# A graph network on one core: the loaded rows of a dense pair added by VectorE in PSUM instead of by a matmul, the output constant added in VectorE's copy

## What is computed

```python
h = jnp.maximum(_layernorm(x, axis=-1), 0.0)
x = x + _L0_gnn_ref(h, ...)      # three graph convolutions and a product
h = jnp.maximum(_layernorm(x, axis=-1), 0.0)
x = x + _L1_gnn_ref(h, ...)      # mean of edges, two products with batch norms
h = jnp.maximum(_layernorm(x, axis=-1), 0.0)
x = x + _L2_gnn_ref(h, ...)      # six steps x += relu(mean of neighbours @ W.T + b)
h = jnp.maximum(_layernorm(x, axis=-1), 0.0)
x = x + _L3_gnn_ref(h, ...)      # tanh(graph convolution) @ W2 + b2
```

## Time and profile before

| | us |
|---|---|
| median of three runs | 3292.27 |
| lowest and highest | 3290.51, 3295.48 |
| the profiled execution | 3287.36 |
| its span | 3285.6 |

### The profile page before, as it was taken

The page is one execution under the profiler, slowest core; times in us unless marked ns, Lnnn a source line. Parts: engine busy times, 40 slices in busy tenths (PEclk is TensorE's granted clock), DMA queues, the critical chain, the costliest instruction groups (busy, mean ns, idle before and its releaser), DMA issues. The chain is left out here.

```text
span 3285.6 us, 46019 instructions
## 1 busy us (share of the span) xinstructions
PE 2527.2 (77%) x11251; PEld 1564.2 (48%) x11251; DVE 2032.4 (62%) x7784; ACT 1972.3 (60%) x4381; POOL 1442.2 (44%) x1507
## 2 busy tenths in 40 slices
PE   5767755558777678899999945799999999876840
PEld 2444434435555456445455422365655656543520
DVE  6544555558889766233333356687887878776630
ACT  1666755557777766455555558877777776764400
POOL 5555454545645264000000000176766767554576
PEclk8888877789888898899999966899999999987875
DMA  4655533445566565333333458866656656433311
GB/s 94 173 158 154 170 109 111 121 119 163 165 179 195 173 193 168 108 137 134 137 134 134 137 183 268 282 186 185 192 177 189 186 175 191 146 116 112 96 57 41
DMA packets 528965, 504.91 MB, mean 154 GB/s; under 512 B 58706, under 2 KB 389955, under 8 KB 528616
## 3 DMA queue, kind: packets, MB, share of 16 engines
q1 hardware_dynamic: 477388, 415.73, 39.2%
q0 software_dynamic: 47184, 85.73, 10.5%
q10 hardware_dynamic: 4172, 0.99, 0.2%
HBM read 246.45 MB, written 260.27 MB: 154 GB/s over the span
## 5 line engine op out<-in xcount | busy, mean ns | idle before, releaser
L1854 POOL DMA_INDIRECT h_G<-step_tab,row_i x294 | 287.1, 977 | 350.1 <-DMA step_tab<-l_NR 192.9
L1854 POOL DMA_INDIRECT h_M<-step_tab,row_i x294 | 284.3, 967 | 119.3 <-issue 86.3
L1567 DVE TENSOR_SCALAR b_Y<-b_BP,col 128x512 f32<-128x512 f32 x148 | 109.9, 742 | 354.5 <-PE b_BP L1521 354.5
L804 PE MATMUL a_PA<-a_H,w 128*128 128x512 f32 x504 | 263.2, 650 | 70.2 <-ACT a_H L968 63.4
L1549 ACT ACTIVATE b_Z<-b_BQ,bn 128x512 f32<-128x512 f32 x148 | 115.0, 777 | 256.7 <-PE b_BQ L1513 256.4
L1521 PE MATMUL b_BP<-b_Z,w 128*128 128x512 f32 x592 | 266.3, 592 | 0.0
L1609 POOL TENSOR_TENSOR b_d<-b_d,neghalf 128x1 f32<-128x1 f32 x1 | 0.6, 565 | 592.4 <-DVE b_d L1600 592.4
L2221 DVE TENSOR_TENSOR_SCAN h_T<-keep,h_T,h_P 128x512 f32<-128x512 bf16 x196 | 222.9, 1137 | 11.3 <-PE h_P L1972 2.1
L270 POOL DMA_INDIRECT h_G<-msg_tab,row_i x147 | 143.8, 978 | 195.5 <-issue 132.1
L239 ACT ACTIVATE a_NR<-a_XR,a_ln_nm,a_ln_rs 128x128 f32<-128x128 f32 x392 | 155.9, 485 | 106.3 <-DVE a_ln_nm L222 106.3
L239 ACT ACTIVATE a_HI<-a_X,a_ln_nm,a_ln_rs 128x128 f32<-128x128 f32 x490 | 201.0, 484 | 23.2 <-DVE a_ln_nm L222 23.2
(11 more groups left out here) (385 smaller groups left out, 6503.9 us busy)
## 6 DMA issues: line engine op xcount, KB each, us to landing
b_HI<-hin_tab SPq DMA_DIRECT2D x148, 256.0 KB, 2.8
y_tab<-b_Y SPq DMA_DIRECT2D x148, 256.0 KB, 2.0
l_Y<-y_tab SPq DMA_DIRECT2D x148, 256.0 KB, 4.0
l_X<-x_tab SPq DMA_DIRECT2D x148, 256.0 KB, 4.6
x_tab<-a_X SPq DMA_DIRECT2D x112, 256.0 KB, 4.3
hin_tab<-a_HI SPq DMA_DIRECT2D x112, 256.0 KB, 3.1
a_XR<-in_x SPq DMA_DIRECT2D x97, 256.0 KB, 4.5
out_rows<-l_O SPq DMA_DIRECT2D x97, 256.0 KB, 3.1
```

Of the source, the lines that this page charges most:

```text
L804: nc.tensor.matmul(PA[b][:, 0:nt * P], w[:, :], h[b][:, 0:nt, :].rearrange("p t d -> p (t d)"), start=True, stop=True).then_inc(done, 1)
L1567: nc.vector.tensor_scalar(Y[b][:, :], BP[b][:, :], col[:, C_B12:C_B12 + 1], None, ALU.add).then_inc(b_y, 1)
L1854: pool.indirect_dma_start(out=GR_[i % 2][b][:, k, :], out_offset=None, in_=table[:, :], in_offset=bass.IndirectOffsetOnAxis(ap=row_i[:, t ...
```

## The change

PE no longer adds the loaded rows and the output constant for dense pairs. `add_x1` and `rows_const` go (a matmul of 128x512 floats and a bf16 matmul for each of 98 banks). In `x2(j)` DVE now adds `X1` to the bank in place, one 128x512 `tensor_tensor` a bank that reads and writes PSUM, after `turned` and `x1_in`, and raises `x2_bank` itself; PE's later matmuls go on adding to the bank. In `rows_out` the copy becomes a `tensor_tensor` that adds a resident broadcast `rb32` of `b32`. `rb32` is loaded at the start by one more DMA in ACT's queue.

```diff
--- before.py
+++ after.py
@@ -141,6 +141,7 @@
     col = sb(top, "col", [P, 12])
     C_B01, C_B02, C_B31, C_B12, C_GA2, C_BE2, C_B11, C_GA1, C_BE1 = 0, 1, 2, 3, 4, 5, 6, 8, 10
     rbh = sb(top, "rbh", [P, D])
+    rb32 = sb(top, "rb32", [P, D])
     split_x1 = sb(top, "split_x1", [3, 512], BF16)
     split_out = sb(top, "split_out", [3, 512], BF16)
     split_r6 = sb(top, "split_r6", [3, 512], BF16)
@@ -494,7 +495,7 @@
     feat_in, feat_pad, mh_st, mh_ones = sems("feat_in", 2), sem("feat_pad"), sems("mh_st", 2), sem("mh_ones")
     FULL = NT - 1
     REST = E - FULL * P
-    N_LOADS = 29
+    N_LOADS = 30
     padded = [(t, base) for t in (hin_tab, x1_tab) for base in (E0, S0)]
     padded += [(t, base) for t in msg_tab[1:] + step_tab + [last_tab] for base in (0, RR)]
 
@@ -917,6 +918,7 @@
         def _(act):
             loads = [(w3[:, :], W03[:, :]), (wl[:, :], W0l[:, :]), (whs[:, :], Wh[:, :]), (b3col[:, :], column(b03)), (bhcol[:, :], column(bh)),
                      (rbl[:, :], b0l.partition_broadcast(P)), (rbh[:, :], bh.partition_broadcast(P)),
+                     (rb32[:, :], b32.partition_broadcast(P)),
                      (w01[:, :], W01[:, :]), (w02[:, :], W02[:, :]),
                      (w31[:, :], W31[:, :]), (w32[:, :], W32[:, :]), (w11[:, :], W11[:, :]),
                      (w12[:, :, :], W12.rearrange("(c p) n -> p c n", p=P)),
@@ -1913,12 +1915,6 @@
                             last = nc.tensor.transpose(turned_in(j, b)[:, k * P:(k + 1) * P], Y[j % 2][b][:, k, :], ident[:, :])
                     last.then_inc(turned, 1)
 
-            def add_x1(j):
-                for b in range(2):
-                    pe.wait_ge(x1_in[j % 2][b], 16 * (j // 2 + 1))
-                    nc.tensor.matmul(XB[j % 2][b][:, :], ident[:, :], X1[j % 2][b][:, :, :].rearrange("p t d -> p (t d)"), start=False,
-                                     stop=True, skip_group_check=True).then_inc(x2_bank, 1)
-
             def x3(j):
                 for b in range(2):
                     if full(j, b):
@@ -1946,17 +1942,13 @@
                     pe.wait_ge(h_set, n + 1)
                     nc.tensor.matmul(PC[b][:, :], w31[:, :], HT[b][:, :, :].rearrange("p t d -> p (t d)"), start=True, stop=True).then_inc(p1_set, 1)
 
-            def rows_const(j):
-                for b in range(2):
-                    nc.tensor.matmul(XB[j % 2][b][:, :], ones3[:, :], split_out[:, :], start=False, stop=False, skip_group_check=True)
-
             def rows(j):
                 for b in range(2):
                     n = 2 * (j - D0) + b
                     pe.wait_ge(tanh_set, n + 1)
                     pc_user[b] = (tanh_set, n + 1)
                     for k in range(4):
-                        last = nc.tensor.matmul(XB[j % 2][b][:, k * P:(k + 1) * P], HT[b][:, k, :], w32[:, :], start=False, stop=(k == 3), skip_group_check=True)
+                        last = nc.tensor.matmul(XB[j % 2][b][:, k * P:(k + 1) * P], HT[b][:, k, :], w32[:, :], start=False, stop=True, skip_group_check=True)
                     last.then_inc(p2_set, 1)
 
             def hop_turn(i):
@@ -2011,8 +2003,6 @@
                 j, its = sl.pair, sl.its
                 if j is not None:
                     turn(j)
-                    if is_d(j):
-                        add_x1(j)
                 if j is not None and MIX < j <= D0:
                     x3(j - 1)
                 for i in its[:1]:
@@ -2020,8 +2010,6 @@
                 if late is not None:
                     turn2(late)
                     prod(late)
-                if late is not None:
-                    rows_const(late)
                 for i in its[:1]:
                     if i < F0:
                         hop_blocks(i, (0,))
@@ -2153,11 +2141,13 @@
         def _(dve):
             def x2(j):
                 for b in range(2):
-                    if is_d(j):
-                        continue
                     q, r, n = 2 * j + b, j % 2, width(j, b)
                     dve.wait_ge(turned, q + 1)
                     dve.wait_ge(x1_in[r][b], 16 * (j // 2 + 1))
+                    if is_d(j):
+                        bank = XB[r][b][:, :].rearrange("p (t d) -> p t d", d=D)
+                        nc.vector.tensor_tensor(bank, X1[r][b][:, :, :], bank, ALU.add).then_inc(x2_bank, 1)
+                        continue
                     if full(j, b):
                         if j >= 2 and full(j - 2, b):
                             dve.wait_ge(x3_sum, no2(j - 2, 0) + no2(j - 2, 1) + (b + 1 if j - 2 > MIX else 1))
@@ -2191,7 +2181,8 @@
                     r = j % 2
                     dve.wait_ge(p2_set, 2 * (j - D0) + b + 1)
                     dve.wait_ge(o_st[b], o_stores(j, b))
-                    nc.vector.tensor_copy(O[b][:, :, :].rearrange("p t d -> p (t d)"), XB[r][b][:, :]).then_inc(o_set, 1)
+                    nc.vector.tensor_tensor(O[b][:, :, :], XB[r][b][:, :].rearrange("p (t d) -> p t d", d=D),
+                                            rb32[:, :].unsqueeze(1).broadcast_to([P, 4, D]), ALU.add).then_inc(o_set, 1)
 
             def rstd2(j):
                 j2 = j - MIX
```

## The result

| | us |
|---|---|
| changed kernel, median of 12 runs | 3300.26 (3290.73 to 3306.73) |
| kernel before, median of 12 runs beside it | 3290.70 (3286.74 to 3298.97) |
| ratio, 95% interval | 1.0023 (1.0013 to 1.0033) |
| span of the profiled execution | 3302.2 (before 3285.6) |

The change costs 0.23%, some 8 us; the forecast was +3.7. How the profile divides it matters more than the total. Busy time by stretch of the changed kernel: sweeps 2 to 5, sweep 6, and the last sweep up to POOL's last long wait (the wait before the 64th gather of that sweep, in both kernels), to be read beside the earlier trace rows.

What follows compares the result with a forecast made beforehand. Prediction: POOL's gather pace plus one turn-around bounds sweeps 1 to 5, the compute chain the last two. Terms -1 + 1.1 + 1.6 + 2 = +3.7 us on 3292.3 gave 3296 us, range 3285 to 3313.

Steps and rivals of the forecast that it cites:

- running past it: Total time: the forecast's own shifts and clock losses exceed its 6.6 us band, giving 3299 to 3306 us; chance 0.15.
- sign of being wrong: Forecast is wrong if sweeps change by over 1 us each, or the last two sweeps' clock by over 0.05.
- POOL's pace bounds the sweeps: Sweeps 2 to 5: POOL's 17.6 us a slot plus one turn-around make 138.5 us; PE's chain takes 17.36 a slot.
- rival 1: DVE becomes the sweeps' bound: 3355 us if adds cost in full, 3305 at 1.7 us a pair; chance 0.09.
- Costs of the pieces: Per pair: PE loses 2.26 us, DVE's two adds take 1.28, the copy about 683 ns; the load costs 0.
- cushion: Slots of sweeps 1 to 5: about 0.15 us a slot left between the compute chain's 17.46 us and POOL's 17.6.
- Sweeps 1 to 5, -1 us: PE's removed work covers the adds' 1.28 us; 0.2 us less at each sweep's end; bounds -2.5 and +39.
- Rival 2: PE's clock falls inside the sweeps as its busy share drops to about 83%: 17 us more, 3313 us; chance 0.11.
- Sweep 6, +1.1 us: Adds on the path in slots 3 and 4, 1.28 us each, less 1.5 for the constant in slots 1, 2, 5.
- +2 us taken for the clock: Last two sweeps: longer PE waits bring extra slow-clock stretches in six pair slots; bounds 0 and +12.
- The last sweep, +1.6 us: F_SLOT +0.6, two slots where PE waits for DVE's `h_G` +1.5 together, the last slot -0.5.
- Rival 3: PE is what is late in the last two sweeps; 7 slots gain 2.26 us: -16 us, 3276 us; chance 0.11.

Runs made afterwards that it cites:

- e4_relief: Changed kernel without DVE's in-place adds, so the dense pairs' rows are left out of the sum; 3285.06 us, ratio 0.9989.
- e3_add: Kernel before with only the dense pair's add moved from PE to DVE; constant stays on PE, no extra load; 3306.17 us, ratio 1.0052.
- e1_load: Kernel before plus only the extra table in SBUF and its load; 3289.48 us, ratio 1.0000.
- e11_pad_again: e3_add plus one unread matmul a block in add_x1's place on PE, on a chip of usual speed; 3299.26 us, ratio 1.0021.
- e2_const: Kernel before plus the load, with the output constant moved from PE to DVE's copy; add_x1 stays on PE; 3283.47 us, ratio 0.9985.
- e6_double: Changed kernel with DVE's in-place add done twice, on a slow chip; 3673.20 us, ratio 1.0158.
- e5_pad: e3_add plus one unread matmul a block in add_x1's place on PE, on a slow chip; 3629.78 us, ratio 1.0024.

## Why the prediction came out as it did

The time, 3300 us, lies in the range; the forecast of 3296 was 4 us low, and its chance sat on "within 6.6 us", which the measured 3300 just leaves for the next class, "running past it". That it came so near is in part luck. It had -1 us for sweeps 1 to 5, where the profiles give +6.5, and +4.7 for the last two sweeps with the clock, where they give +0.1: two errors of opposite sign. Its own sign of being wrong, sweeps that change by more than 1 us each, came true (1.3 us each). By its own steps:

- **POOL's pace bounds the sweeps, with PE 2% behind.** Right. With 49 us less of PE's busy time sweeps 2 to 5 got no shorter (e4_relief), and rival 1's 3355 us didn't come: with 38 us more on DVE, already the fullest engine after PE, they took 4.4 us longer (7.3 in e3_add). That speaks against the rule of the Trainium skill (Perfetto Trace Analysis, Identifying the Most-Contended Engine) weighed there.
- **Costs of the pieces.** Right: adds 687 ns against 683, copy 682 against 683, the load 0 (e1_load 1.0000), the chain 17.39 us against 17.46. DVE's idle time ahead of the first hop's affine fell from 1.34 to 0.17 us. PE's share in sweeps 2 to 5 fell only to 86%, not 83%, since part of its work ran at the half clock. The upper bound of +39 us left out the cushion that the text had itself found: less 0.15 us in each of 35 slots it is +34.
- **Sweeps 1 to 5, -1 us.** Wrong, and the step is the cover: the text took the chain for slot by slot faster than POOL, and asked only what it costs per slot. It is the restart of a sweep that decides, since a late start is made up at only 0.2 us a slot. The profiles give 691.5 before and 698.0 after, +6.5 us (+2.9 to +9.2 in the other kernels with adds).
- **Rival 2, the clock inside the sweeps.** The clock did fall there, to 0.97, and the loss is a good third of its price of 17 us; that the clock alone caused it isn't shown. The "against" reckoned with a PE that is evenly less busy. In mid-sweep, behind the first 23 us of a sweep, the clock does stay at 1.00 in 24 of 25 stretches of 23 us (PE busy for 81 to 91% of them). The falls lie at the start, in the slot without a hop and the one behind it, where the text had no row. The Trainium skill (TensorE: Matmul & The Clock Gate, What's actually happening) has the clock depend on activity; the trace agrees, 0.93 us busy of 3.00 and then 1.2 GHz.
- **Rival 1, DVE as the bound.** Its point of decision, adds of over 1.45 us, was not reached, and the cushion was real (17.39 against 17.6). Yet it lost its use as a reserve: e11_pad_again, with PE's work of before, still takes 2.9 us more than before in sweeps 1 to 5, though the larger part of its loss lies in the last two sweeps.
- **Sweep 6, +1.1 us.** Right in sign, small in both terms. e2_const shows the constant's relief at 2.4 us (1.5 taken; 3.6 against e1_load), and against e2_const the adds cost 4.4 (2.56 taken). Net +2.1. The clock of sweep 6 fell from 0.81 to 0.77; how much of the 2.1 us that is, and so of the +2 us taken for the clock, isn't parted.
- **The last sweep, +1.6 us.** Not found: 99.39 us against 101.37 up to POOL's last long wait. The wait of PE for DVE's `h_G` did grow as worked out, 2.52 to 5.21 us (5.5 forecast), so the mechanism is there. The clock of the stretch is 0.87 both times, so no loss of clock shows in it. Together the two last sweeps take 291.9 us, as before (291.8), against a forecast of 293 to 298. The step that was mis-sized is the constant's relief: 1.5 us in sweep 6 and some 1.6 (three times 0.54) in the last sweep were taken, and 5 to 9 us were found over both, while the adds' two times 2.56 us agree with the 5 to 6.5 found.
- **Rival 3, PE late in the last two sweeps, -16 us.** For the constant it holds in part, 5 to 9 us over the two sweeps. For add_x1 it doesn't: e4_relief without any add has 187.5 us in sweep 6, 0.6 less than e2_const.

PE's timeline in the last sweep of the changed kernel shows that last wait, and the transposes behind it at the low clock (1.73 us, 1.01 before):

```profile
3054.14 1.73 PE L1964 MATMUL h_P<-ident,h_G 128*128 128x128 f32 x7 [5.21 <-DVE h_G L2203]
```

So the +8 us are: sweeps 1 to 5 about +6, of which some 3 are left when PE gets its work back (e11_pad_again); the last two sweeps about 0 in the sum, a gain from the constant given back by the adds; and 2 us that the profiles do not place, less than their scatter. How the sweeps' loss divides between the emptier PE and the later DVE is not settled: both make the start of a sweep later, and the two sweeps shown above that had only one of them lost nothing.

## What to carry to other kernels

Before taking work from an engine that is nearly full but not the limit, look for the place where its pipeline restarts: there that work may be what keeps its clock up (as it may where the engine comes to wait for its input, as in e4_relief), and a delay at the start of a loop stays until the loop's slack has made it up, here 0.2 us a slot. A change of two parts should be timed in parts: the constant in DVE's copy alone gives 0.9985 (0.9974 to 0.9997), the add in PSUM alone 1.0052 (1.0038 to 1.0065), and together they hide each other. The constant cost DVE nothing in a pass that it makes anyway (682 ns with and without it); the new pass takes 1.28 us of DVE's time a pair.

## What was not expected of the hardware

- The kernel before took some 3290 us in three sets of runs, and 3579 and 3623 us on two other chips. There sweeps 1 to 5 take 164 to 180 us each in place of some 138.5 (e6_double left out), POOL waits 21 to 27 us between them in place of 13 to 14, and DVE is idle for something that the trace calls remote, 2.8 us at a time on average in e5_pad, ahead of one instruction in a slot. The cause wasn't looked into; no ratio measured there was used for the sweeps' loss.
- Work whose result nobody reads made a kernel faster: e3_add with 1.9 us of unread matmuls a slot, 1.0052 to 1.0021, each against the kernel before on its own chip.
- An add that reads and writes the same PSUM bank took 687 ns for 128x512 floats, 4 ns more than one that writes SBUF.
